# Softmax denominators inverted two steps later, row maxima transposed one step later, finished values copied ahead of projections

## What is computed

```python
qkv = x @ w_in.T + b_in                      # x: (4, 1024, 256)
q, k, v = (to_heads(t) for t in jnp.split(qkv, 3, axis=-1))   # 16 heads of 16
scores = jnp.einsum('bhqd,bhkd->bhqk', q * scale, k) + causal_bias
attn = jax.nn.softmax(scores, axis=-1)
out = jnp.einsum('bhqk,bhkd->bhqd', attn, v)
out = merge_heads(out) @ w_out.T + b_out
x = layernorm(x + out)
```

## Time and profile before

| | |
|---|---|
| median of the timed runs | 2405.68 us (3 runs, 2405.28 to 2407.26) |
| profiled execution | 2410.23 us, span 2408.4 us |
| busy share of the span: PE, DVE, ACT, POOL | 87%, 60%, 50%, 32% |
| mean granted PE clock | 0.948 |
| first self-attention | up to about 818 us of the span |
| denominators to inverses, DMA to landing (median) | 1.6 us for the load of dens, 2.6 us for those of rden |

### The profile page before, as it was taken

The page is one execution under the profiler, slowest core; times in us unless marked ns, Lnnn a source line. Parts: engine busy times, 40 slices in busy tenths (PEclk is TensorE's granted clock), DMA queues, the critical chain, the costliest instruction groups (busy, mean ns, idle before and its releaser), DMA issues. The chain is left out here.

```text
span 2408.4 us, 33268 instructions
## 1 busy us (share of the span) xinstructions
PE 2086.6 (87%) x11559; PEld 1184.7 (49%) x11586; DVE 1446.7 (60%) x2698; ACT 1214.8 (50%) x2773; POOL 767.5 (32%) x1082
## 2 busy tenths in 40 slices
PE   6888899889998689999999986989899967788887
PEld 3333344344343445565555554556566643445445
DVE  4665566466773265666887975565744345557645
ACT  2455445544646265566887860757532324354342
POOL 4251220220010200121543541574642322443333
PEclk8899899999999899999999998989999988899898
DMA  6445333433421200000110104100001166544320
GB/s 153 111 74 138 79 64 87 85 76 65 73 56 38 65 21 5 28 27 9 62 51 34 51 34 181 40 7 27 9 29 48 49 123 115 127 92 93 75 67 34
DMA packets 132520, 156.60 MB, mean 65 GB/s; under 512 B 36493, under 2 KB 102929, under 8 KB 132258
## 3 DMA queue, kind: packets, MB, share of 16 engines
q1 hardware_dynamic: 132354, 154.47, 26.8%
HBM read 107.55 MB, written 46.86 MB: 64 GB/s over the span
## 5 line engine op out<-in xcount | busy, mean ns | idle before, releaser
L531 ACT ACTIVATE pbuf_sb<-psB 128x512 f32<-128x512 f32 (+1 forms) x608 | 330.1, 573 | 288.1 <-PE psB L409 238.5
L717 DVE TENSOR_REDUCE negm_sb<-psA 128x1 f32<-128x640 f32 (+6 forms) x352 | 352.3, 1027 | 187.9 <-PE psA L397 180.7
L1258 ACT ACTIVATE pw_sb<-psA,nmx_sb 128x154 f32<-128x154 f32 x512 | 191.9, 389 | 133.6 <-DVE nmx_sb L1403 133.6
L406 PE MATMUL psB<-qst_sb,kst_sb 99*128 99x512 bf16 (+3 forms) x768 | 238.8, 341 | 16.8 <-issue 5.1
L395 PE MATMUL psA<-kst_sb,qst_sb 96*128 96x512 bf16 (+3 forms) x768 | 202.9, 341 | 23.8 <-DVE negm_sb L717 22.7
L1403 DVE TENSOR_REDUCE nmx_sb<-psA 128x4 f32<-128x616 f32 x128 | 101.9, 796 | 125.1 <-PE psA L1027 124.9
L423 PE MATMUL psO<-pbuf_sb,V_sb 128*32 128x512 f32 (+3 forms) x1536 | 166.8, 515 | 11.0 <-ACT OT_sb L517 8.9
L406 PEld LDWEIGHTS psB<-qst_sb,kst_sb 99*128 99x128 bf16 x768 | 76.3, 100 | 182.2 <-ACT pbuf_sb L531 129.1
L2919 DVE TENSOR_REDUCE negm_sb<-psA 128x2 f32<-128x320 f32 x256 | 116.1, 481 | 72.0 <-PE psA L2682 67.5
L2802 ACT ACTIVATE pb_sb<-psB 128x512 f32<-128x512 f32 x160 | 92.8, 601 | 131.8 <-PE psB L2692 128.6
L2449 DVE TENSOR_REDUCE nma_sb<-psA 128x1 f32<-128x1024 f32 x32 | 39.1, 1222 | 142.4 <-PE psA L2046 142.4
(11 more groups left out here) (308 smaller groups left out, 4568.9 us busy)
## 6 DMA issues: line engine op xcount, KB each, us to landing
qst_sb<-parts_dram SPq DMA_DIRECT2D x192, 128.0 KB, 4.6
rden_sb<-dens_dram SPq DMA_DIRECT2D x128, 128.0 KB, 2.6
parts_dram<-parts_sb SPq DMA_DIRECT2D x32, 384.0 KB, 2.9
kst_sb<-parts_dram SPq DMA_DIRECT2D x96, 128.0 KB, 7.5
x_dram<-X_sb SPq DMA_DIRECT2D x64, 128.0 KB, 1.7
y_dram<-yw_sb SPq DMA_DIRECT2D x16, 512.0 KB, 2.8
Y_sb<-y_dram SPq DMA_DIRECT2D x16, 512.0 KB, 9.1
parts_dram<-partsb_sb SPq DMA_DIRECT2D x16, 384.0 KB, 3.0
```

The lines of the kernel that those rows point to most:

```text
L406: last = nc.tensor.matmul(psB[:, k, at:at + hi - lo], kst[0:MAX_ROWS, gg % 3, h, i * P:(i + 1) * P], qst[0:MAX_ROWS, gg % 3, h, lo:hi], st ...
L531: nc.scalar.activation(pbuf[:, key % 2, heads[0]:heads[-1] + 1, lo:hi], psB[:, (nb.n - 1) % 2, 0:len(heads) * (hi - lo)] .rearrange("p (h ...
L717: nc.vector.tensor_reduce(out=negm[:, gg % 2, heads[0]:heads[-1] + 1, j], in_=psA[:, (na.n - 1) % 2, :].rearrange("p (h n) -> p h n", h=le ...
L1258: last = nc.scalar.activation(pw[:, m % 2, h, :], psA[:, m % 2, at:at + K], ACT.Exp, bias=nmx[:, m % 2, h:h + 1], accum_out=psx[:, m % 3, ...
```

## The change

Four things are moved; no instruction is added or taken away.

- SP's `reciprocals` is cut in two: `denominators` (store, wait, load) stays in unit 8m+3 behind the stack loads; `inverses` (wait for the reciprocal, store, wait, four loads) goes to unit 8m+7, behind the DMAs of the maxima. DVE takes the reciprocal in its unit 8m+6 instead of 8m+4, POOL scales in its unit 8m+8 instead of 8m+5.
- The transposition of the maxima goes from the end of a group's last unit into the next unit, behind its first second score and the values of half 1; DVE's `split_max` goes to the head of that unit.
- The output projections move from kk 16 to 23 to kk 18 to 25.
- ACT's `copy_out` is queued ahead of `store_qk` in a unit that has both.

```diff
--- before.py
+++ after.py
@@ -207,7 +207,7 @@
     def out_unit(k):
 
         b, kk = k // 32 - 1, k % 32
-        return (b, kk - 16) if 0 <= b < B - 1 and 16 <= kk < 24 else None
+        return (b, kk - 18) if 0 <= b < B - 1 and 18 <= kk < 26 else None
 
     def early_groups(k):
 
@@ -252,12 +252,15 @@
                                      parts_dram[b % 2, qk, part, g * 4 * HD:(g + 1) * 4 * HD, :]
                                      .rearrange("(h d) n -> d h n", d=HD)).then_inc(stack_loaded[gg % 3], 16)
 
-            def reciprocals(gg):
+            def denominators(gg):
 
                 sp.wait_ge(o_free, 2 * (gg + 1))
                 sp.dma_start(dens_dram[0], OT[HD:P:32, gg % OTN, :]).then_inc(dens_stored, 16)
                 sp.wait_ge(dens_stored, 16 * (gg + 1))
                 sp.dma_start(dens[:, :], dens_dram[0].rearrange("h (a n) -> (h a) n", a=P // 4)).then_inc(dens_loaded, 16)
+
+            def inverses(gg):
+
                 sp.wait_ge(inv_made, gg + 1)
                 sp.dma_start(dens_dram[1].rearrange("h (a n) -> (h a) n", a=P // 4), dens[:, :]).then_inc(inv_stored, 16)
                 sp.wait_ge(inv_stored, 16 * (gg + 1))
@@ -325,20 +328,23 @@
                         parts_landed(8 * ((gg + 1) // G + 1))
                     load_stack(gg + 1)
                 if early_groups(k) is not None:
-                    reciprocals(early_groups(k))
+                    denominators(early_groups(k))
                 if k < UNITS and k % 8 == 7:
                     sp.wait_ge(maxparts_made, gg + 1)
                     sp.dma_start(max_dram[gg % 2].rearrange("a r n -> r a n"), mpart[:, gg % 2, :, :]).then_inc(maxparts_stored, 16)
                     sp.wait_ge(maxparts_stored, 16 * (gg + 1))
                     sp.dma_start(qst[QK_ROWS:MAX_ROWS, gg % 3, :, :],
                                  max_dram[gg % 2].rearrange("a (h j) n -> a h (j n)", h=4)).then_inc(maxrows_loaded, 16)
+                if early_groups(k - 4) is not None:
+                    inverses(early_groups(k - 4))
                 if k >= 2 and out_unit(k - 2):
                     store_tile(*out_unit(k - 2))
                 if k < UNITS and kk == 28:
                     if b > 0:
                         sp.wait_ge(x_stored, 16 * NT * b)
                     sp.dma_start(X0[:, :, :], t["x"][b].rearrange("(n p) d -> p n d", p=P)).then_inc(x_loaded, 16)
-            reciprocals(G * B - 1)
+            denominators(G * B - 1)
+            inverses(G * B - 1)
             for j in range(NT):
                 store_tile(B - 1, j)
             sp.wait_ge(x_stored, 16 * NT * B)
@@ -426,6 +432,13 @@
                                             stop=(i == (0, 4)[c]), tile_position=(0, 32 * h), skip_group_check=True)
                 if c == 0 or i > 3:
                     last.then_inc(pv_done, 1)
+
+            def transpose_maxima(gg):
+
+                pe.wait_ge(a_free, na.n)
+                a = slot_a()
+                nc.tensor.transpose(psA[0:32, a, 0:P], negm[:, gg % 2, :, :].rearrange("p h j -> p (h j)"),
+                                    ident[:, :]).then_inc(a_full, 1)
 
             pe.wait_ge(first_loaded, 16)
             for u in range(8):
@@ -452,6 +465,8 @@
                         first_scores(k // 8, first[f], query_tile(k))
                     if u == 0 and s >= 1:
                         values((s - 1) // 8, KEY_ORDER[(s - 1) % 8], exps_at[s - 1], 1)
+                    if u == 0 and k % 8 == 0 and 8 <= k <= UNITS:
+                        transpose_maxima(k // 8 - 1)
                     if u == 1 and s >= 1:
                         values((s - 1) // 8, KEY_ORDER[(s - 1) % 8], exps_at[s - 1], 0)
                 exps_at[s] = nb.n
@@ -467,11 +482,6 @@
                     pe.wait_ge(summed, 2)
                     a = slot_a()
                     nc.tensor.matmul(psA[:, a, 0:2], ones[:, :], asum[:, :], start=True, stop=True).then_inc(a_full, 1)
-                if k < UNITS and k % 8 == 7:
-                    pe.wait_ge(a_free, na.n)
-                    a = slot_a()
-                    nc.tensor.transpose(psA[0:32, a, 0:P], negm[:, (k // 8) % 2, :, :].rearrange("p h j -> p (h j)"),
-                                        ident[:, :]).then_inc(a_full, 1)
                 if v_unit(k):
                     project_v(*v_unit(k))
                 if out_unit(k):
@@ -531,13 +541,13 @@
                         nc.scalar.activation(pbuf[:, key % 2, heads[0]:heads[-1] + 1, lo:hi],
                                              psB[:, (nb.n - 1) % 2, 0:len(heads) * (hi - lo)]
                                              .rearrange("p (h n) -> p h n", h=len(heads)), ACT.Exp).then_inc(b_free, 1)
-                if qk_unit(k):
-                    store_qk(*qk_unit(k))
                 if s >= 0:
                     if i == 0 and gg > 0:
                         copy_out(gg - 1, 1)
                     if i == 5:
                         copy_out(gg, 0)
+                if qk_unit(k):
+                    store_qk(*qk_unit(k))
             copy_out(G * B - 1, 1)
 
         @block.gpsimd
@@ -619,8 +629,8 @@
                     split_qk(*qk_unit(k))
                 if 18 <= k < 30 and k % 2 == 0:
                     quantise((k - 18) // 2)
-                if k >= 2 and early_groups(k - 2) is not None:
-                    scale_values(early_groups(k - 2))
+                if early_groups(k - 5) is not None:
+                    scale_values(early_groups(k - 5))
                 if out_unit(k):
                     inverse_deviation(*out_unit(k))
             for j in range(NT):
@@ -708,6 +718,8 @@
                 nc.vector.reciprocal(rs1[:, :], m1[:, :]).then_inc(m1_ready, 1)
 
             for k in range(LAST + 1):
+                if k % 8 == 0 and 8 <= k <= UNITS:
+                    split_max(k // 8 - 1)
                 if k < UNITS:
                     gg, j = k // 8, query_tile(k)
                     if gg >= 2 and k % 8 == 0:
@@ -722,10 +734,8 @@
                         sum_weights(k - W_AT + 3)
                     if k == W_AT:
                         weight_scales()
-                    if k % 8 == 7:
-                        split_max(gg)
-                if early_groups(k - 1) is not None:
-                    reciprocals(early_groups(k - 1))
+                if early_groups(k - 3) is not None:
+                    reciprocals(early_groups(k - 3))
                 if v_unit(k):
                     take_v(*v_unit(k))
                 if k % 32 == 12 and 1 <= k // 32 < B:
```

## The result

The kernel after takes 2380.44 us (median of 4 runs, 2375.77 to 2384.84), beside 2405.65 us for the kernel before, measured next to it; the ratio is 0.9892, 95% interval 0.9876 to 0.9908. It is faster by 25 us, where 53 were forecast, and lies above the upper end of the range, 2376. A second comparison gave 0.9912 (0.9898 to 0.9925). The profiled execution took 2384.8 us with a span of 2383.0; that of before had 2408.4.

A forecast was written before the change was run, and what follows sets the result against it. It took TensorE with short holes as the bound, plus stalls beside projections in the first self-attention. Gains 38.0 + 1.6 + 13.1 + 4.1 = 56.8 less costs 3.5 gave net 53.3 us: 2352 us from 2405.7, range 2343 to 2376.

The forecast's parts named there:

- The four reciprocal stalls: Units 37, 45, 69, 77: VectorE waits about 7 us for denominators, PE 2.7 to 5.4; moving reciprocals later removes them.
- The transposition: Moving it into the next unit shrinks PE's 1.32 us hole by 0.87 in 15 groups: 13.1 us, bounds 0 to 19.8.
- The copy: ScalarE's copy ahead of the store removes PE's 1.68 us hole before the values, at no cost; counted in the excess.
- the 38.0: Excess time of four eight-unit stretches with query/key projections over clean ones, all taken as gain; bounds 16 and 41 us.
- The cast of unit 24: A 0.21 us cast takes 3.19 us behind GpSimd's L613; scaling queued later frees it: gain 4.1 us, bounds 0 and 4.1.
- What the moved steps cost: Costs of SP's longer queue and displaced units in the first self-attention: 0.6 + 1.4 + 1.5 = 3.5 us.
- the output projection: Scaled values at R+12.6 (R: end of first scores in a group's last unit) tie with PE: 0.6 us, bounds 0 and 12.
- the input load: Next batch's input queues behind SP's inverse DMAs, out at R+8.4, PE asks at R+13.3: 1.4 us, bounds 0 and 8.
- units 24 and 25: With both V and output projections, PE can meet a slot VectorE still reads: 1.5 us in all, bounds 0 and 4.
- Rival (a): SP's chain is late: DMA slowed 4 us, three output projections and two input loads wait, 20 us: 2372; chance 0.17.
- (d): Maxima's two DMAs, with 1.8 us to spare, land late; 15 groups wait 7 us each: slower, 2457; chance 0.03.
- (e): Denominators land later still, VectorE meets the same wait two units on, nothing gained: 2406; chance 0.04.

The follow-up runs named there:

- reciprocals alone: Kernel before with only the reciprocals, SP's cut, scaling and output projections moved two units later, transposition and copy left as before: 2386.09 us, 0.9928 to before.
- the repaired kernel: Kernel after plus scaling two GpSimd steps later, input load issued before the inverses, output projections at kk 19 to 26: 2353.51 us (0.9797 to before), again 2354.46 (0.9796).

## Why the prediction was wrong

**The gains.** They are there. The four reciprocal stalls vanished with their low clock. The transposition was forecast at 13.1 us. The medians of the experiment that undoes it say 15.2. Its trace says 15.0 in the last units of the groups, more than the forecast's 0.87 a group because the cover beside a projection is longer, as the bounds had named, and 3.6 given back elsewhere, so 11.4; the intervals of the two ratios leave room for both, and the term was right in size. The copy was worth 6 to 7 us, but only with the reciprocals moved, so counting it within the 38.0 was right and counting it by itself would have been wrong. The cast of unit 24 takes 0.21 us now. The 4.1 us for it were the top of the draw: against the 4.1 us that unit 24 takes in "reciprocals alone", the two traces of before have 4.1 and 0.7 us more.

What was over-sized is the sum as a whole. By unit 127 the repaired kernel's second trace is 56.4 us ahead of the first trace of before, close to the forecast's 56.8; against the second trace of before it is 43.3. The medians say 48.6 (2403.0 to 2354.5), between the two, as the one trace of before is long and the other short. I had taken the profiled span as 4.5 us long, from its distance to the timed median, and read all excess times from it as they stood. This is worth up to 8 us (56.8 less 48.6), some of it at the start (below).

**The step that failed is "What the moved steps cost".** It gave 0.6 us for the output projection, 1.4 for the input load and 1.5 for units 24 and 25, 3.5 in all. The comparison of the kernel after with the repaired one prices the three at 27.3 us. So 23.8 of the 28 us that are missing are here. The rest, 4 us by this count and 8 by the second comparison (whose medians are 21.2 us apart), is in the sum above. One by one:

- Input load: 11.6 us instead of 1.4. SP's part was right for unit 34: the load goes out 8.7 us after R (forecast 8.4), and PE goes on 5.0 us later. For unit 66 it was 9.2 and the landing took 6.3. What was wrong is when PE asks. I took R+13.3. But it asks at R+11.2 and R+11.6, and the trace of before had it: in batch 2,

```profile
400.92 0.28 PE L473 MATMUL psA<-ident_sb,negm_sb 128*32 128x128 f32 x1 [1.32 <-DVE negm_sb L717]
...
411.92 1.50 PE L364 MATMUL psB<-xT_sb,wqkv_sb 128*128 128x512 f32 x3
```

  R is 399.60, PE asks at R+12.3, less the 0.87 that it now runs ahead: R+11.5. I had read the time from batch 0, whose units contain a wait of 2.1 us for max_dram that the same paragraph forecast to vanish.
- Output projection: together with the next term 15.7 us instead of 2.1. The scaled values came at R+13.8 to R+14.3, not R+12.6, and PE asked at R+12.8, R+12.8 and R+11.1, not 14.4, 14.4 and 12.6 (by the forecast's own rows, R+1.66 and 11.2 us, the last should have read 12.9). The two errors are of about one size, 1.2 to 1.7 us for the values and 1.5 to 1.6 for the asking. I had used a stretch between two first scores of a unit. A unit's queue does not end there: the projection is its last entry, and the next unit's second scores, which come before its first scores, lie behind it. PE reaches the projection about 2 us before the stretch ends.
- The chain to the scaled values, in the timeline of SP of the kernel after:

```profile
377.51 0.26 SPq L336 DMA_DIRECT2D qst_sb<-max_dram  x1
377.82 0.34 SPq L265 DMA_DIRECT2D dens_dram<-dens_sb  x1
379.90 1.71 SPq L270 DMA_DIRECT2D rden_sb<-dens_dram  x4
381.70 0.40 SPq L314 DMA_DIRECT2D xT_sb<-xT  x1
```

  The inverses' store is issued 0.31 us behind the maxima's load, and its reader 2.08 us after it, where 1.44 was measured for the same DMA with nothing ahead of it. The maxima's load itself went out at R+4.3 to R+5.4. Rival (a), the chain on SP late, is half of what happened: the chain was late by 1 to 2 us and not by 4 (for unit 34 by nothing), and PE asked 1.5 to 2.1 us early. There were eight places instead of five, and in each trace the clock fell behind five of them. That its 2372 is nearer than the forecast is partly luck.
- Units 24 and 25: I feared a second reader of a slot. The real wait was that VectorE's normalisation needs two short POOL instructions queued behind the scaling. `scale_values`, moved three units down, now stands ahead of the inverse deviation of an output tile and waits there for the inverses. I had walked SP's queue in this way and not POOL's.

**The clock.** I gave the removed holes of 1.32 us no clock, and that holds: the plain groups stand at 1.00 with them and without them. I gave the new waits none either, and that failed. Of the 27.3 us some 10.8 are PE at 0.50. This is how much longer PE is busy with the same work in the second trace of the kernel after: 1.8 and 2.9 us in units 34 and 66, behind holes of 2.56 and 4.30 us, and 1.7, 1.6 and 2.8 us in units 58, 90 and 122, behind holes of 0.57, 1.56 and 1.86 us (in units 58 and 90 with one of 0.67 us close behind).

**Small points.** (d) did not happen at its size, but its 1.8 us to spare are not there either: PE waits for the maxima 2.0 us in four places (0.7 at most). (e) did not happen. The start: the wait in unit 9 for the maxima of group 0 is 7.26 us, not 5.08: PE comes 6.3 us earlier, and the wait ends 4.2 us earlier. Over the traces of the changed kernels it lies between 5.4 and 11.5 us. This part of the saving is lost, as forecast. And from unit 127 (30.8 us ahead) to the end (25 ahead) the kernel after loses some 5 us to before in stages that the change does not touch. The two traces of the unchanged kernel drift against each other by some 4 us in the same stages (20.6 us apart at 1670 us, 16.4 at the end), so I put it down to the draw; no run isolates it.

## What to carry to other kernels

When a step in an in-order queue is moved, list for each queue everything that now stands behind it, and for each of these who waits for it: a tiny instruction behind a long wait stopped two engines here. Time the moment at which a consumer asks by the consumer's own instruction in an undisturbed repetition, not by the end of a stretch, and take 1 to 2 us of slack as none, because PE can pay for a missed one twice, in idle time and in clock. And a part that is worth nothing alone may be worth its full size when the next wait is removed, so judge parts within the combination.

## What the runs showed of the hardware that I had not expected

- The granted clock after a hole: 3.4 us of PE at 0.50 after one of 2.56 us, 5.1 us after one of 3.81. After holes of 1.5 us (units 50 and 82) it stayed at 1.00. A hole of 2.75 us in unit 114 was followed by a fall (mean 0.84 over the unit), one of 2.70 us at the same place in the second trace was not (1.00).
- Two short holes 0.7 us apart can do the same: 1.36 and 0.67 us in unit 90 were followed by a fall (mean 0.81), and so were 0.57 and 0.67 us in unit 58 of the second trace (0.80), while 0.40 and 0.67 us there in the first trace were not (1.00). The Trainium skill, "TensorE: Matmul & The Clock Gate", section "A second HAM failure mode: psum-queue depth-cycling", speaks of short, frequent idles between groups of matmuls. These pairs agree with it. The 16 holes of 1.32 us, one in each group, are short but not frequent, and the clock stays at 1.00 in the plain groups.
- A small store issued directly behind a load takes 2.0 to 2.3 us to its reader, where it took 1.4 alone; behind the input load it took 4.7 (201.43 to 206.09 in the repaired kernel).
- Two profiled executions of one program differed by 16.4 us in the span, where the medians of the comparisons that they belong to are 2405.7 and 2400.7 us; the ten runs of the second spread over 15.8 us.
